# A state-space stage on Trainium2: the three-way split of the C rows done by GpSimd instead of by VectorE

## The chip, the cores and the metric

The kernel runs on one core of a Trainium2 chip. The metric is the device time of one execution in microseconds. TensorE, VectorE, ScalarE and GpSimd each work through their own list of instructions; SyncE (SP) issues the transfers between HBM and the on-chip memory SBUF. The engines meet only at semaphores.

## The reference

The program is a decoder of four layers with twelve blocks, over 128 sequences of 64 rows of 128 numbers. The change lies in one block, the attention slot of layer 2, which is a two-way state-space model ("mamba"), one pass forward and one over the reversed sequences. One pass is

```python
xz = einsum('bld,ed->ble', x, in_w); xs, z = split(xz, 2)
xs = silu(conv(xs) + conv_b)                       # 4 taps
dt, Bc, Cc = split(einsum('bld,ed->ble', xs, xproj_w), [8, 24])
dt = softplus(einsum('blr,dr->bld', dt, dt_w) + dt_b)
A = -exp(Alog)
dA  = exp(dt[..., None] * A)                       # 16 states
dBx = dt[..., None] * Bc[:, :, None, :] * xs[..., None]
h[t] = dA[t] * h[t-1] + dBx[t]
y[t] = sum over the states of h[t] * C[t]
out = ((y + Dp * xs) * silu(z)) @ out_w.T
```

## The kernel before

The stage is the function `mamba`. It treats 512 rows (eight sequences) at a time, called a group, with the 256 inner channels as two halves of 128 partitions. There are 16 groups to a pass and two passes, so 32 groups in one run of loops; `par` is the parity of a group. `group` on each engine goes over the states s = 3 to 15 of group i and then over states 0 to 2 of group i + 1; beside the states of group i, the preparation (`front`) of group i + 1 is done a piece at a time.

For each state GpSimd multiplies dt * xs (`dtx`) by the state's row of B, spread over all partitions, into `dBx` (`state`, L2602 to L2612; the multiplication is at L2600). ScalarE makes the decays exp(dt * A) (L2824), one of the two halves at a time, in three slots of PSUM. VectorE runs the recurrence over both halves (`scan`, L2957 to L2966), and multiplies the result by the row of C (`weigh`, L2976). TensorE spreads the row of C over the partitions in `ps_C` (L2700), and adds up the weighed states in `ps_y` (L2719). `dBx` has four slots: GpSimd waits before state s until state s - 4 is scanned. ScalarE may be three halves ahead of the scan.

The C rows reach TensorE as three bf16 parts whose sum is the fp32 row, so that the product with a matrix of ones and zeros is exact in bf16. The way is: ScalarE writes the low-rank products `low` (L2855, at its state 5); SP stores them in HBM (L2532) and loads the C rows as `piece`, 128 partitions of 64 (L2535); `split_rows` forms the three parts (L2947 to L2955); SP stores them (L2539) and loads them as `parts` (L2542); TensorE first needs them for state 0 of the next group, in its step of state 15. SP's order for a group is: store and load of the rows (`store_rows`), B rows of the state pairs 0 and 1, the parts (`load_parts`), B rows of the pairs 2 to 7 (`spread_B`, each of which waits for GpSimd's products).

`SPLIT` is 8. VectorE does, in its group i, scan 8, weigh 7, and then `split_rows(i + 1)`, then scan 9.

GpSimd's `front` for group i + 1 adds x and ln at s = 11 (L2620, waiting for ScalarE's ln of L2870), then v + e (L2624), v * r, dt + v (L2630) and dtx, each behind the product of a state. The sequence on ScalarE that leads to it is: relu and exp after the decays of state 8 (L2863, L2865), v and ln after the decays of state 9 (L2868, L2870). At the first state of the next group VectorE needs GpSimd's first product, which needs dtx.

Between the two passes (`turnover`) VectorE also scales the other pass's taps (L2927) after state 10 of one group, and makes two diagonal matrices (L2932) after state 10 of the next.

Of the kernel before, what the change touches and what calls it, by code (L numbers as in the profile page):

```python
# [66 lines left out]
class Scope:  # L67
# [15 lines left out]
    def sb(self, name, shape, dt=F32):  # L83
        if name in self.weights:
            return self.weights[name]
        return self.ctx.enter_context(self.nc.sbuf_tensor(f"{self.name}_{name}", shape, dt))
# [4 lines left out]
    def sem(self, name):  # L91
        self.sems.append(self.nc.alloc_semaphore(name=f"{self.name}_{name}"))
        return self.sems[-1]


def bc(ap, shape):
    return ap.to_broadcast(shape)
# [1216 lines left out]
def rows(t, i):  # L1314

    return t[:, bass.ds(i * TPG, TPG), :]
# [1147 lines left out]
def mamba(C, name, W, BC_rows, part_rows):  # L2464
# [5 lines left out]
    nc = C.nc  # L2470
# [5 lines left out]
    SKIPPED, SPLIT, PIECE = 6, 8, NS * GT // P  # L2476
    FREE_HALVES, FREE_STATES, FREE_ROWS = 3, SLOTS * CHUNK, 1
    with ExitStack() as ctx:
# [16 lines left out]
        piece, rest, split = sb("piece", [P, PIECE]), sb("rest", [P, PIECE]), sb("split", [P, 3, PIECE], BF16)  # L2495
# [12 lines left out]
        dbl_done, piece_loaded, split_ready = sem("dbl_done"), sem("piece_loaded"), sem("split_ready")  # L2508
# [80 lines left out]
        @block.gpsimd  # L2589
        def _(pool):  # L2590
            nc.gpsimd.memset(hT[:], 0.0).then_inc(prepared, 1)
            nc.gpsimd.memset(dBx[:], 0.0).then_inc(dBx_ready, FREE_STATES)
            pool.drain()

            def hold():

                pool.sem_inc(begun, 1)

            def multiply(to, one, other):
                return nc.gpsimd.tensor_tensor(to, one, other, ALU.mult)  # L2600

            def state(j, s, par, in_prologue=False):  # L2602

                slot = s // CHUNK % SLOTS
                if s % CHUNK == 0:
                    pool.wait_ge(B_loaded[slot], j * 32 + (s // FREE_STATES * 16 + 16))
                if s >= BX or not in_prologue:
                    pool.wait_ge(scanned, j * (2 * NS) + (2 * s - 2 * BX + 2 + FREE_HALVES))
                hold()
                halves = lambda t: t.rearrange("p m t -> p t m")  # L2610
                multiply(halves(dBx[:, s % BX, :, :]), halves(dtx[:]),
                         bc(Bs[:, slot, s % CHUNK, :].unsqueeze(2), [P, GT, NHF])).then_inc(dBx_ready, 1)  # L2612

            def front(j, s, par):


                if s == 11:
                    pool.wait_ge(ln_ready, j + 1)
                    hold()
                    nc.gpsimd.tensor_tensor(dt[:, par, :, :], x[:], ln[:], ALU.add)  # L2620
                elif s == 12:
                    pool.wait_ge(excess, j + 1)
                    hold()
                    nc.gpsimd.tensor_tensor(v[:], v[:], e[:], ALU.add)  # L2624
                    pool.drain()
                elif s == 13:
                    multiply(v[:], v[:], r[:])
                    pool.drain()
                elif s == 14:
                    nc.gpsimd.tensor_tensor(dt[:, par, :, :], dt[:, par, :, :], v[:], ALU.add).then_inc(dt_ready, 1)  # L2630
                    pool.drain()
                elif s == 15:
                    pool.drain()
                    multiply(dtx[:], dt[:, par, :, :], xs[:, par, :, :])
                    pool.drain()

            for s in range(11, 16):
                front(0, s, 0)
            for s in range(AHEAD):
                state(0, s, 0, True)  # L2640
            with pool.Fori(0, C.NG) as pair:
                for par in range(2):
                    i = pair * 2 + par
                    for s in range(AHEAD, NS):
                        state(i, s, par)
                        front(i + 1, s, 1 - par)
                    for s in range(AHEAD):
                        state(i + 1, s, 1 - par)
# [271 lines left out]
        def _(dve):  # L2920
# [3 lines left out]
            def scale_taps():  # L2924

                for k in range(NTAP):
                    last = nc.vector.tensor_tensor(taps[:, k, :], taps[:, k, :], in_w[:, 0:DI], ALU.mult)  # L2927
                return last

            def diagonals(second):  # L2930
                for m in range(NHF):
                    last = nc.vector.tensor_scalar(diagD[:, m, :], C.ident[:], Dp[:, second, m:m + 1], None, ALU.mult)  # L2932
                return last
# [10 lines left out]
            nc.vector.tensor_scalar(A[:], A[:], -1.0, None, ALU.mult).then_inc(prepared, 1)  # L2944
            dve.drain()

            def split_rows(j):  # L2947

                dve.wait_ge(piece_loaded, j * 16 + 16)
                nc.vector.tensor_copy(split[:, 0, :], piece[:])  # L2950
                dve.drain()
                nc.vector.tensor_tensor(split[:, 1, :], piece[:], split[:, 0, :], ALU.subtract)
                nc.vector.tensor_tensor(rest[:], piece[:], split[:, 0, :], ALU.subtract)
                dve.drain()
                nc.vector.tensor_tensor(split[:, 2, :], rest[:], split[:, 1, :], ALU.subtract).then_inc(split_ready, 1)  # L2955

            def scan(j, s, in_prologue=False):  # L2957
                if s >= HS or not in_prologue:
                    weighed = (s - HS) % NS
                    back = 1 if s < HS else 0  # L2960
                    dve.wait_ge(yc_ready, j * NDW + (weighed + 1 - back * NDW + FREE_ROWS))
                dve.wait_ge(dBx_ready, j * NS + (s + 1 + FREE_STATES))
                for m in range(NHF):
                    dve.wait_ge(decay, j * (2 * NS) + (2 * s + m + 1))
                    nc.vector.tensor_tensor_scan(hs[:, s % HS, m, :], ps_dA[:, (2 * s + m) % 3, :], dBx[:, s % BX, m, :], 0.0,  # L2965
                                                 ALU.mult, ALU.add).then_inc(scanned, 1)  # L2966

            def weigh(j, s, wait_free=True):
                if s in POOL_WEIGHS:
                    return  # L2970
                rank = DVE_WEIGHS.index(s)
                dve.wait_ge(scanned, j * (2 * NS) + (2 * s + NHF + FREE_HALVES))
                if wait_free:
                    dve.wait_ge(y_added, j * NS + (DVE_WEIGHS[rank - 2] + 1 - (NS if rank < 2 else 0)))
                dve.wait_ge(C_done, j * NDW + (rank + 1))
                nc.vector.tensor_tensor(yc[:, rank % 2, :, :], hs[:, s % HS, :, :], bc(ps_C[:].unsqueeze(1), both),  # L2976
                                        ALU.mult).then_inc(yc_ready, 1)

            split_rows(0)
            for s in range(AHEAD):  # L2980
                scan(0, s, True)
                if s:
# [2 lines left out]
            def group(i, par, second, turnover=False):  # L2985

                for s in range(AHEAD, NS):
                    scan(i, s)
                    weigh(i, s - 1)
                    if s == SPLIT:  # L2990
                        split_rows(i + 1)
                    if turnover and par == 0 and s == SPLIT + 2:
                        dve.wait_ge(taps_loaded, 32)
                        scale_taps().then_inc(taps_ready, 1)
                    if turnover and par == 1 and s == SPLIT + 2:
                        dve.wait_ge(y_added, i * NS + (SKIPPED + 1))
                        diagonals(1).then_inc(diag_ready, 1)
                scan(i + 1, 0)
                weigh(i, NS - 1)
                scan(i + 1, 1)  # L3000
                dve.wait_ge(y_added, i * NS + NS)
                nc.vector.tensor_tensor(q[:], sz[:, par, :, :], ps_y[:], ALU.mult).then_inc(y_ready, 1)
                weigh(i + 1, 0)
                scan(i + 1, 2)
                weigh(i + 1, 1)
                dve.wait_ge(out_done, i + 1)
                if not second:
                    dve.wait_ge(Y_ready, i + 1)
                at = rows(C.Y, i - SECOND if second else i)
                nc.vector.tensor_tensor(at, ps_j[:].rearrange("p (t d) -> p t d", d=D), at, ALU.add).then_inc(out_read, 1)  # L3010

            with dve.Fori(*LOOPS[0]) as pair:
                for par in range(2):
                    group(pair * 2 + par, par, False)
            for par in range(2):
                group(SECOND - 2 + par, par, False, True)
# [1277 lines left out]
```

## Time and profile before

| what | value |
|---|---|
| median of three runs | 7302.22 us (7290.1 to 7309.01) |
| span of the profiled execution | 7292.4 us |
| the stage of the change | about 2290 to 4160 us of the span, 32 groups |
| busy share of the whole span | TensorE 89%, VectorE 74%, ScalarE 56%, GpSimd 39% |

The profile is of one execution. For each instruction the trace has its start, its duration, its line and its tiles, and the idle time of its engine before it with what ended it. POOL is GpSimd, DVE is VectorE, ACT is ScalarE, PE is TensorE and SPq is the DMA queue of SP. The tiles of the stage are named with m_ in front. "issue" is a wait for nothing that the profile shows.

### The profile page before, as it was taken

Reading aid. Unit: us, or ns where it says so; the run is one execution under the profiler, and the core shown is the slowest. Engines: PE = TensorE matmul, PEld = TensorE weight load, DVE = VectorE, ACT = ScalarE, POOL = GpSimd, SP = SyncE. Lnnn points to the kernel's source line nnn. Section 1 sums busy time; section 2 is a strip of 40 time slices with the busy share of each in tenths; the row PEclk is TensorE's granted clock in tenths of the full one; section 3 lists DMA queues with packets and bytes.
Section 4 is the critical chain, followed back from the end, with each engine's and each line's share of the span. In section 5 each row is a group of like instructions: output and inputs, shape, how many; then the busy total and the mean of one; then the engine's idle time right before and its main releaser. Section 6 shows DMA issues by size and latency. Waiting matters only on the chain. (4 is left out here: it accounts for less than half of the span.)

```text
span 7292.4 us, 189527 instructions
## 1 busy us (share of the span) xinstructions
PE 6507.4 (89%) x74836; PEld 3973.7 (54%) x74836; DVE 5360.5 (74%) x8933; ACT 4055.2 (56%) x6024; POOL 2820.5 (39%) x1680
## 2 busy tenths in 40 slices
PE   7989987887697989989999779989899999989998
PEld 5767665444442333333333356666576767667676
DVE  7877576665556999999999856677577777768544
ACT  3556343665446777777777745455344444456433
POOL 3321175332214888888888601165021212211000
PEclk9999978999888999999999989999999999999999
DMA  1000000000001222222222100000000000000000
GB/s 29 0 21 13 3 11 8 3 3 2 14 2 52 76 73 75 75 80 77 76 75 76 51 12 13 9 31 3 12 2 2 2 2 2 2 15 14 2 0 23
DMA packets 115881, 190.04 MB, mean 26 GB/s; under 512 B 38661, under 2 KB 74746, under 8 KB 114970
## 3 DMA queue, kind: packets, MB, share of 16 engines
q1 hardware_dynamic: 112218, 183.47, 7.9%
q8 instruction: 337, 5.52, 0.3%
q10 hardware_dynamic: 3264, 0.54, 0.1%
q14 instruction: 62, 0.51, 0.0%
HBM read 173.87 MB, written 7.98 MB: 25 GB/s over the span
## 5 line engine op out<-in xcount | busy, mean ns | idle before, releaser
L2600 POOL TENSOR_TENSOR m_dBx<-m_dtx,m_Bs 128x1024 f32<-128x1024 f32 x515 | 1165.8, 2283 | 227.3 <-DVE m_hs L2965 185.2
L2965 DVE TENSOR_TENSOR_SCAN m_hs<-m_ps_dA,m_dBx 128x512 f32<-128x512 f32 x1030 | 1200.5, 1207 | 56.4 <-POOL m_dBx L2600 55.8
L2719 PE MATMUL m_ps_y<-m_yc,ident 128*128 128x512 f32 x2060 | 1021.6, 619 | 0.0
L2824 ACT ACTIVATE m_ps_dA<-m_dt,m_A 128x504 f32<-128x504 f32 x1030 | 682.0, 678 | 427.1 <-DVE m_hs L2965 424.4
L2096 POOL TENSOR_TENSOR a_s<-a_s,a_den 128x1024 f32<-128x1024 f32 x128 | 243.5, 1902 | 1123.9 <-DVE a_den L2142 1123.9
L2976 DVE TENSOR_TENSOR m_yc<-m_hs,m_ps_C 128x1024 f32<-128x1024 f32 x515 | 616.3, 1197 | 1.3 <-PE m_ps_C L2700 1.3
L2719 PEld LDWEIGHTS m_ps_y<-m_yc,ident 128*128 128x128 f32 x2060 | 350.5, 190 | 357.0 <-issue 357.0
L2700 PE MATMUL m_ps_C<-m_parts,m_sel 48*128 48x512 bf16 x516 | 199.8, 387 | 175.7 <-DVE m_yc L2976 175.6
L2700 PEld LDWEIGHTS m_ps_C<-m_parts,m_sel 48*128 48x128 bf16 x516 | 47.7, 92 | 566.9 <-DVE m_yc L2976 421.2
L625 POOL TENSOR_TENSOR c_kbd<-c_kf,c_hmask 128x1024 f32<-128x1024 f32 x66 | 125.0, 1893 | 515.9 <-ACT c_kf L534 492.0
L2140 DVE TENSOR_REDUCE a_den<-a_s 128x16 f32<-128x1024 f32 x128 | 156.0, 1219 | 207.0 <-ACT a_s L2047 207.0
L1930 PEld LDWEIGHTS a_ps_out<-a_wo,a_oT 128*128 128x128 f32 x2048 | 238.3, 192 | 102.9 <-ACT a_oT L2051 102.9
L1653 PEld LDWEIGHTS f_ps_o<-f_w,f_hid 128*128 128x128 f32 x2048 | 246.4, 192 | 66.0 <-issue 46.1
L1930 PE MATMUL a_ps_out<-a_wo,a_oT 128*128 128x128 f32 x2048 | 261.0, 281 | 10.8 <-ACT a_oT L2051 1.1
L1682 ACT ACTIVATE f_hid<-f_ps_h 128x1024 f32<-128x1024 f32 x128 | 129.4, 1023 | 247.7 <-PE f_ps_h L1644 247.5
L2096 POOL TENSOR_TENSOR c_s<-c_s,c_den 128x1024 f32<-128x1024 f32 x32 | 60.9, 1902 | 514.3 <-DVE c_den L2142 514.3
L1730 DVE SCALAR_TENSOR_TENSOR f_acc<-f_ps_o,f_cw,f_acc 128x128 f32<-128x128 f32 x384 | 108.1, 344 | 203.7 <-PE f_ps_o L1653 203.7
L1653 PE MATMUL f_ps_o<-f_w,f_hid 128*128 128x128 f32 x2048 | 250.9, 276 | 7.2 <-ACT f_hid L1682 7.2
L1644 PE MATMUL f_ps_h<-f_xnT,f_w 128*128 128x512 f32 x512 | 241.6, 600 | 0.0
L2043 ACT ACTIVATE a_pT<-a_ps_t 128x1024 f32<-128x1024 f32 x128 | 130.7, 1021 | 141.4 <-PE a_ps_t L1905 141.4
L3732 POOL TENSOR_TENSOR x_qk<-x_qk,x_spread 128x1024 f32<-128x1024 f32 x36 | 85.2, 2367 | 307.7 <-ACT x_spread L3607 307.7
L2027 ACT ACTIVATE a_qT<-a_ps_j 128x512 f32<-128x512 f32 x129 | 77.0, 597 | 219.6 <-PE a_ps_j L1860 219.5
(748 smaller groups left out, 16025.2 us busy)
## 6 DMA issues: line engine op xcount, KB each, us to landing
m_Bs<-BC_rows SPq DMA_DIRECT2D x258, 512.0 KB, 3.5
c_kvb<-in_ctxT SPq DMA_DIRECT2D x68, 128.0 KB, 2.1
c_kvb<-in_ctxT SPq DMA_DIRECT2D x17, 256.0 KB, 2.7
out_dram<-X SPq DMA_DIRECT2D x1, 4096.0 KB
BC_rows<-m_low SPq DMA_DIRECT2D x33, 64.0 KB, 2.7
part_rows<-m_split SPq DMA_DIRECT2D x33, 48.0 KB, 1.7
m_parts<-part_rows SPq DMA_DIRECT2D x33, 48.0 KB, 1.7
m_piece<-BC_rows SPq DMA_DIRECT2D x33, 32.0 KB, 1.7
```

Of the source, the lines that this page charges most:

```text
L1644: last = nc.tensor.matmul(ps_h[:, e % 2, c, :], w1[:, e, c * P:(c + 1) * P], fr.xnT[:], start=True, stop=True)
L1653: last = nc.tensor.matmul(ps_o[:, e % 2, p * D:(p + 1) * D], hid[:, e % 2, c, p * P:(p + 1) * P], w2[:, e, c, :], start=(c == 0), stop=(c ...
L1930: last = nc.tensor.matmul(ps_out[:, UT * u + t, :], oT[:, t, j, :], wo[:, t, hg * NJ + j, :], start=hg == 0 and u == 0 and t == 0 and j == ...
L2043: nc.scalar.activation(pT[:].rearrange("p t j q -> p t (j q)"), ps_t[:], ACT.Copy).then_inc(pT_ready, 1)
L2096: nc.gpsimd.tensor_tensor(s1[:, par, :, :, :], s1[:, par, :, :, :], bc(den[:, par, :, :].unsqueeze(3), [P, UT, UH, S]), ALU.mult).then_inc ...
L2140: nc.vector.tensor_reduce(den[:, par, :, :], s1[:, par, :, :, :], AX, ALU.add)
L2600: return nc.gpsimd.tensor_tensor(to, one, other, ALU.mult)
L2700: nc.tensor.matmul(ps_C[:], sel[0:3 * NS, s, :], parts[0:3 * NS, par, :], start=True, stop=True).then_inc(C_done, 1)
L2719: last = nc.tensor.matmul(ps_y[:, m, :], C.ident[:], of[:, m, :], start=s == 0, stop=s == NS - 1)
L2824: nc.scalar.activation(seqs(ps_dA[:, h % 3, :]), seqs(dt[:, par, m, :]), ACT.Exp, scale=A[:, second, m, s:s + 1]).then_inc(decay, 1)
L2965: nc.vector.tensor_tensor_scan(hs[:, s % HS, m, :], ps_dA[:, (2 * s + m) % 3, :], dBx[:, s % BX, m, :], 0.0, ALU.mult, ALU.add).then_inc(s ...
L2976: nc.vector.tensor_tensor(yc[:, rank % 2, :, :], hs[:, s % HS, :, :], bc(ps_C[:].unsqueeze(1), both), ALU.mult).then_inc(yc_ready, 1)
```

## The change

The function `split_rows` goes from VectorE's block to GpSimd's, with the same four operations, now with `hold()` (an increment of a semaphore that nobody waits for) behind its wait. VectorE's calls, one before the loops and one after weigh 7 of each group, are removed. GpSimd calls it before its first work and, in each group, in `front` at s = 8, that is behind its product of state 8 and ahead of that of state 9. `SPLIT` stays 8; as GpSimd is ahead of VectorE by up to four states, the place is another moment in time.

```diff
+            def split_rows(j):
+
+                pool.wait_ge(piece_loaded, j * 16 + 16)
+                hold()
+                nc.gpsimd.tensor_copy(split[:, 0, :], piece[:])
+                pool.drain()
+                nc.gpsimd.tensor_tensor(split[:, 1, :], piece[:], split[:, 0, :], ALU.subtract)
+                nc.gpsimd.tensor_tensor(rest[:], piece[:], split[:, 0, :], ALU.subtract)
+                pool.drain()
+                nc.gpsimd.tensor_tensor(split[:, 2, :], rest[:], split[:, 1, :], ALU.subtract).then_inc(split_ready, 1)
+
             def front(j, s, par):
 
-
+                if s == SPLIT:
+                    split_rows(j)
                 if s == 11:
...
+            split_rows(0)
             for s in range(11, 16):
                 front(0, s, 0)
...
-            def split_rows(j):
-
-                dve.wait_ge(piece_loaded, j * 16 + 16)
-                nc.vector.tensor_copy(split[:, 0, :], piece[:])
-                dve.drain()
-                nc.vector.tensor_tensor(split[:, 1, :], piece[:], split[:, 0, :], ALU.subtract)
-                nc.vector.tensor_tensor(rest[:], piece[:], split[:, 0, :], ALU.subtract)
-                dve.drain()
-                nc.vector.tensor_tensor(split[:, 2, :], rest[:], split[:, 1, :], ALU.subtract).then_inc(split_ready, 1)
-
...
-            split_rows(0)
             for s in range(AHEAD):
                 scan(0, s, True)
...
                     weigh(i, s - 1)
-                    if s == SPLIT:
-                        split_rows(i + 1)
```

## Rows read from the trace of the kernel before

**Rows 1.** The page's costliest groups: line, engine, operation, tiles, count, busy, mean, idle before.

```profile
L2600 POOL TENSOR_TENSOR m_dBx<-m_dtx,m_Bs 128x1024 f32<-128x1024 f32 x515 | 1165.8, 2283 | 227.3 <-DVE m_hs L2965 185.2
L2965 DVE TENSOR_TENSOR_SCAN m_hs<-m_ps_dA,m_dBx 128x512 f32<-128x512 f32 x1030 | 1200.5, 1207 | 56.4 <-POOL m_dBx L2600 55.8
```

**Rows 2.** Busy time by engine in ten stretches of the stage, their sum.

```profile
sum 1860.00, PE 1687.38 PEld 656.88 DVE 1809.77 ACT 1420.13 POOL 1530.40; mean PE 168.74 PEld 65.69 DVE 180.98 ACT 142.01 POOL 153.04
```

**Rows 3.** Waits of VectorE, 2290 to 4150: total us, times, longest.

```profile
DVE m_hs L2965 <- POOL m_dBx L2600: 37.1, 30, 1.3
```

**Rows 4.** Timeline, VectorE, one group: start, duration, instruction, count, idle before.

```profile
3009.70 2.33 DVE L2965 TENSOR_TENSOR_SCAN m_hs<-m_ps_dA,m_dBx 128x512 f32<-128x512 f32 x2
...
3013.06 0.19 DVE L2950 CAST m_split<-m_piece 128x64 bf16<-128x64 f32 x1
...
3013.95 2.34 DVE L2965 TENSOR_TENSOR_SCAN m_hs<-m_ps_dA,m_dBx 128x512 f32<-128x512 f32 x2
...
3034.12 2.33 DVE L2965 TENSOR_TENSOR_SCAN m_hs<-m_ps_dA,m_dBx 128x512 f32<-128x512 f32 x2
...
3038.78 2.34 DVE L2965 TENSOR_TENSOR_SCAN m_hs<-m_ps_dA,m_dBx 128x512 f32<-128x512 f32 x2 [1.22 <-POOL m_dBx L2600]
```

**Rows 5.** Timeline, GpSimd, the same group; the first row is state 8.

```profile
2998.85 2.29 POOL L2600 TENSOR_TENSOR m_dBx<-m_dtx,m_Bs 128x1024 f32<-128x1024 f32 x1 [1.15 <-DVE m_hs L2965]
...
3014.19 2.36 POOL L2620 TENSOR_TENSOR m_dt<-m_x,m_ln 128x1024 f32<-128x1024 f32 x1 [3.05 <-ACT m_ln L2870]
...
3036.37 15.68 POOL L2600 TENSOR_TENSOR m_dBx<-m_dtx,m_Bs 128x1024 f32<-128x1024 f32 x7 [0.39 <-issue]
```

**Rows 6.** Timeline, ScalarE, the same group: the decay of state 8 and ln.

```profile
3007.59 0.69 ACT L2824 ACTIVATE m_ps_dA<-m_dt,m_A 128x504 f32<-128x504 f32 x1 [0.92 <-DVE m_hs L2965]
...
3012.95 1.06 ACT L2870 ACTIVATE m_ln<-m_v 128x1024 f32<-128x1024 f32 x1
```

**Rows 7.** Tile m_split, 2290 to 4150: count, duration min/median/max in ns, first and last start.

```profile
L2950 DVE CAST m_split<-m_piece x32: 184/186/191, 2316.5 to 4121.5; 128x64 bf16<-128x64 f32 x32
```

**Rows 8.** Between the passes: all of L2927, then timelines of GpSimd and VectorE.

```profile
L2927 DVE TENSOR_TENSOR m_taps<-m_taps,m_in_w x8: 412/423/2554, 2241.9 to 3140.1; 128x256 f32<-128x256 f32 x8
...
3136.69 5.97 DVE L2927 TENSOR_TENSOR m_taps<-m_taps,m_in_w 128x256 f32<-128x256 f32 x4
...
3139.87 2.51 POOL L2600 TENSOR_TENSOR m_v<-m_v,m_r 128x1024 f32<-128x1024 f32 x1
...
3166.55 1.22 DVE L3002 TENSOR_TENSOR m_e<-m_sz,m_ps_y 128x1024 f32<-128x1024 f32 x1 [0.58 <-PE m_ps_y L2719]
...
3218.62 2.34 DVE L2965 TENSOR_TENSOR_SCAN m_hs<-m_ps_dA,m_dBx 128x512 f32<-128x512 f32 x2 [0.58 <-DVE m_yc L2976]
```

**Rows 9.** Narrow GpSimd instructions of other stages: timeline, and groups of instructions.

```profile
4761.92 0.30 POOL L652 TENSOR_SCALAR f_hidden<-f_seen 128x128 bf16<-128x128 f32 x1 [0.16 <-issue]
...
L1128 POOL TENSOR_TENSOR a_feat<-a_expo,a_above 128x512 f32<-128x512 f32 x34 | 43.2, 1272 | 5.2 <-issue 4.6
...
L647 POOL TENSOR_TENSOR f_seen<-f_seen,f_tril 128x128 f32<-128x128 f32 x34 | 15.6, 457 | 5.2 <-issue 4.4
```

**Rows 10.** The piece: its transfer in two groups, landing times, and the tightest dt addition.

```profile
3001.55 0.33 SPq L2535 DMA_DIRECT2D m_piece<-BC_rows  x1
...
3014.01 0.37 SPq L2539 DMA_DIRECT2D part_rows<-m_split  x1
...
DMA to landing us min/median/max: 1.6/1.7/1.9
...
3587.98 0.32 SPq L2535 DMA_DIRECT2D m_piece<-BC_rows  x1
...
3600.26 2.35 POOL L2620 TENSOR_TENSOR m_dt<-m_x,m_ln 128x1024 f32<-128x1024 f32 x1 [3.03 <-ACT m_ln L2870]
```

**Rows 11.** Timeline ahead of the loops, VectorE's first split and GpSimd's first addition.

```profile
2267.70 0.20 DVE L2950 CAST m_split<-m_piece 128x64 bf16<-128x64 f32 x1 [21.03 <-DMA m_piece<-BC_rows]
...
2272.60 2.35 POOL L2620 TENSOR_TENSOR m_dt<-m_x,m_ln 128x1024 f32<-128x1024 f32 x1 [32.38 <-ACT m_ln L2870]
```

## Prediction

> **What bounds the kernel now.** I read the page first, then the waits of the stage, then one group of the stage instruction by instruction on each engine, and last the few rows that price small GpSimd instructions. The page puts the two costliest GpSimd and VectorE loops of the whole program into this stage [rows 1]. Here VectorE works 1809.8 of 1860 us and GpSimd 1530.4 [rows 2], so VectorE looks like the bound and taking work from it looks like a gain. The waits say something finer: VectorE stands still 37.1 us in 30 places, each time for a dBx that GpSimd has not finished, at most 1.3 us [rows 3]. There are 32 groups; 30 of them hold one such wait.
>
> One group shows where. VectorE runs scan, weigh, scan, weigh without a gap to state 15 (3034.12), and then the next group's state 0 starts at 3038.78 after 1.22 us of waiting for GpSimd [rows 4]. GpSimd's own line shows the opposite pattern [rows 5]: through state 11 it waits about 1.1 us before every product because it may be only four states ahead of the scans; then it waits 3.05 us for ScalarE's ln; and from 3014.19, where ln releases it, it runs dt, v, dtx and the products of states 12 to 15 nearly back to back until dBx of the next group's state 0 is there at 3036.37 + 2.28 = 3038.65. VectorE starts 0.13 us later. So each group has two parts. From the first scan to the first half of state 7's scan VectorE sets the pace. That half releases ScalarE at 3007.59 [rows 6]; two relu, two exp of states, v and ln follow on ScalarE, ln ends at 3014.01, and from there GpSimd's chain of 3038.65 - 3014.19 = 24.5 us sets the pace. VectorE only accompanies that second part and arrives 1.22 us early.
>
> **Where the split stands in this.** On VectorE it begins at 3013.06, after weigh 7, and ends where scan 9 starts at 3013.95 [rows 4]: 0.89 us, four instructions and two drains. That is in the second part, behind scan 7, which releases the path, and beside the path. All 32 groups have it, on average 58.2 us apart ((4121.5 - 2316.5) / 31 [rows 7]).
>
> **Removed.** 32 x 0.89 = 28.5 us of VectorE time in the loop, and 0.9 us ahead of it, in a stretch where VectorE otherwise waits for GpSimd's first products. In an ordinary group scans 9 to 15 come 0.89 us earlier. The latest of the products is dBx 15: counted back from 3036.37 over the gap of 0.39, dtx (2.36 like the addition of 3014.19) and a gap of 0.16 behind a drain, it ends at about 3033.5, and scan 15 would come at 3034.12 - 0.89 = 3033.23, so some 0.3 us of waiting appears there; the earlier products have more room. The next scan cannot start before 3038.65 + 0.13 whatever VectorE does. What is late next is the same GpSimd product as now, only the wait grows from 1.22 to about 2.1 us (shared between scan 15 and the next scan 0). Gain of an ordinary group: 0. The later work of the group (out, Y, weigh 15) comes after that scan on VectorE, so it does not move either.
>
> Two groups are unlike the others, those between the two passes. In one, 5.97 us of tap scaling lengthen VectorE's line and no wait for GpSimd is left; the waits there are short ones for TensorE (0.58 us at 3166.55 [rows 8]), whose convolution waits for these very taps. There the 0.89 us come off the path. The other is about even: the next scan 0, at 3218.62, comes after an idle 0.58 us already, so it has arrived early too. I count 0.9 us in all.
>
> **Added, on GpSimd.** After dBx 8: a wait for the DMA of the piece, one cast, three subtractions of 128x64, two drains. None of these is in the trace on this engine. The nearest rows [rows 9]: a tensor_tensor of 128x128 took 0.457 us and one of 128x512 1.272 us, so 2.12 ns a column and, extrapolated, an estimated 0.32 us at 64 columns; a write of 128x128 into bf16 took 0.298 us, and an instruction behind a drain started 0.16 us late. Hence 3 x 0.32 + 0.30 + 2 x 0.16 = 1.58 us, and 0.39 us for taking up the products again (the largest such gap, [rows 5]): 1.97 us, the value I take. Lower bound: the 0.89 us of VectorE; nothing excludes a drain at no cost but nothing makes four instructions a gain. Upper bound, all four at the 128-column price and three gaps: 4 x 0.457 + 3 x 0.16 + 0.39 = 2.7 us.
>
> **What hides it.** The piece is issued at 3001.55 and lands 1.7 us later (1.9 at most) [rows 10], so at 3003.25; GpSimd is done with dBx 8 at 3001.14 and waits 2.1 us for it. Queued behind this wait are dBx 9, 10 and 11, 3 x 2.28 = 6.85 us, and then the dt addition, due at 3014.19. The split must be over by 3007.35: 4.1 us are free, 2 are wanted. In the tightest groups the piece comes 12.28 us ahead of the dt addition (3600.26 - 3587.98 [rows 10]), and 12.28 - 1.9 - 6.85 = 3.5 us are free. So dBx 9 ends near 3007.5 instead of 3004.4; its reader, scan 9, comes at 3013.06. dBx 11 ends near 3012.1, two microseconds before ln. The cost is hidden by GpSimd's waiting for scans and for ln; if that cover went, each microsecond would cost 32 us. On SP's queue the same transfers go in the same order: B rows of state pair 0 wait for dBx 9 and go 3 us later, those of pair 1 1 us later; the stores and loads of the parts, which waited for VectorE until 3014.01, follow at once and go some 1.5 us earlier. All are wanted only about 3036 or later. ScalarE never waits for dBx. Ahead of the loops the piece is there at 2267.7 and GpSimd's first addition starts at 2272.60 [rows 11]: 2267.7 + 1.97 = 2269.7, 2.9 us to spare.
>
> **VectorE and GpSimd at once.** The split now runs beside scan 6 and weigh 6, in the part that VectorE paces, so a slowdown of the scans would cost there. Rows show that two engines can block each other: the tap scaling, whose two operands both lie in SBUF, takes 0.41 to 0.42 us alone and up to 2.55 us beside GpSimd's products, which themselves go from 2.36 to 2.51 us [rows 8]. But the scan (one operand in PSUM) takes 2.33 to 2.34 us a pair both at 3009.70, half of it beside an idle GpSimd, and at 3034.12, wholly beside a busy one [rows 4]. After the change no VectorE instruction of an ordinary group has two SBUF operands. The Trainium skill says the same (SBUF — State Buffer, section Who interferes with whom): an instruction of VectorE with two SBUF inputs contends with GpSimd's reads, one with at most one does not. The skill also warns (Perfetto Trace Analysis, Optimizing Scalar/DVE Operations) that moving work between these two might not help, as they share a port. Taken at its worst it is the third rival below.
>
> **Sum.** 7292.4 - 0.9 = 7291.5 us in the profiled execution. Its span lies between the lowest (7290.1) and the middle (7302.22) of the three timed runs, so what lies around the span is smaller than their spread and I carry the difference over: 7302.2 - 0.9 = 7301.3 us.
>
> **Rivals.** (1) VectorE is the bound after all, and GpSimd's late product moves up with it. Then 32 x 0.89 = 28.5 us are won: 7273.7. For it: VectorE's 97% in the stage. Against it: the 30 waits for GpSimd, and that GpSimd's chain starts at ln, fixed before the split. Chance 0.08. (2) Slower: the split on GpSimd outlasts the free time, the dt addition comes late, and everything up to the next group's first scan with it. It decides from 3.5 to 4.1 us a group. At 1 us an instruction and 0.16 a drain with 0.39 behind, it is 4.7 to 4.9 us; 0.8 us over, 32 times, gives +26 us: 7328. Against it: instructions of twice the columns take 0.30 and 0.46 us [rows 9]. Chance 0.06. (3) The engines block each other: each of the four instructions holds a scan or weigh up for its 0.32 us, before scan 7: 32 x 1.28 = 41 us: 7343. Against it: the constant scans. Chance 0.06. (4) Forecast, chance 0.80. That the split would not move is no case: the code has it only on GpSimd, and whether it costs GpSimd one microsecond or three, the forecast is the same.
>
> **How the numbers follow.** A measurement of this kernel can tell about 0.3%, 22 us, from no change. Rival 1 passes that on the one side, rivals 2 and 3 mostly on the other; a partial form of each end is left a little: faster 0.09, same 0.79, slower 0.12. The forecast's own range is the spread of the runs, about -11 to +8 us; I widen it toward partial forms of the rivals, 7282 to 7318, leaving out the full rivals.
>
> **What would show it.** The four instructions in GpSimd's line at about 3003 to 3005, 0.3 us each. GpSimd's idle time before the dt addition falls from 3.05 to about 2.1 us; its waits before dBx 9 to 11 vanish. VectorE busy falls by about 27 us while its wait for dBx grows from 37 to some 65 us. The groups stay 58.2 us apart on average. If they are 57.3 apart, rival 1 holds; if the dt addition shows no wait for ln, rival 2; if a scan pair is above 2.33 us near the split, rival 3.

## The result and the profile after

The changed kernel takes 7333.09 us (five runs, 7324.99 to 7339.58) against 7297.25 us (five runs, 7290.1 to 7309.01) for the kernel before on the same chip: ratio 1.0046 [1.0035, 1.0057], some 34 us slower by the ratio and 36 between the medians. The brackets hold the 95% interval; every ratio below is to the kernel before, timed along with that run. The forecast was 7301.3 us, at most 7318. It was wrong: the change costs time where it was expected to cost none.

The changed kernel's page (scan at L2968 now, decays at L2837) shows the instruction queue q14 grown from 62 packets and 0.51 MB in the kernel before (first line here), and the idle time ahead of the scan at 125.5 us where it was 56.4 [rows 1]:

```profile
q14 instruction: 62, 0.51, 0.0%
...
q14 instruction: 96, 0.79, 0.0%
...
L2968 DVE TENSOR_TENSOR_SCAN m_hs<-m_ps_dA,m_dBx 128x512 f32<-128x512 f32 x1030 | 1199.0, 1204 | 125.5 <-POOL m_dBx L2600 95.9
L2600 POOL TENSOR_TENSOR m_dBx<-m_dtx,m_Bs 128x1024 f32<-128x1024 f32 x515 | 1162.6, 2283 | 153.8 <-DVE m_hs L2968 120.6
```

An ordinary group, GpSimd's timeline, answers to [rows 5]:

```profile
3054.78 0.24 POOL L2618 CAST m_split<-m_piece 128x64 bf16<-128x64 f32 x1 [2.44 <-DMA m_piece<-BC_rows]
3055.16 0.30 POOL L2620 TENSOR_TENSOR m_split<-m_piece,m_split 128x64 bf16<-128x64 f32 x1
3055.42 0.30 POOL L2621 TENSOR_TENSOR m_rest<-m_piece,m_split 128x64 f32<-128x64 f32 x1
3055.87 0.30 POOL L2623 TENSOR_TENSOR m_split<-m_rest,m_split 128x64 bf16<-128x64 f32 x1
3056.13 6.76 POOL L2600 TENSOR_TENSOR m_dBx<-m_dtx,m_Bs 128x1024 f32<-128x1024 f32 x3
3065.49 2.36 POOL L2632 TENSOR_TENSOR m_dt<-m_x,m_ln 128x1024 f32<-128x1024 f32 x1 [2.60 <-ACT m_ln L2883]
...
3087.67 13.43 POOL L2600 TENSOR_TENSOR m_dBx<-m_dtx,m_Bs 128x1024 f32<-128x1024 f32 x6 [0.38 <-issue]
```

The split takes 1.35 us with its gaps (3054.78 to 3056.13), the three products behind it are done long before ln, and the dt addition still waits 2.60 us for it. VectorE in the same group, answering to [rows 4]:

```profile
3084.81 2.34 DVE L2968 TENSOR_TENSOR_SCAN m_hs<-m_ps_dA,m_dBx 128x512 f32<-128x512 f32 x2 [0.20 <-POOL m_dBx L2600]
...
3090.08 2.34 DVE L2968 TENSOR_TENSOR_SCAN m_hs<-m_ps_dA,m_dBx 128x512 f32<-128x512 f32 x2 [1.82 <-POOL m_dBx L2600]
```

That is the forecast's picture almost to the tenth. From one dt addition to the next I read 58.0 us in this group, as before. The loss is elsewhere. VectorE's waits from 2290 to 4150 us, answering to [rows 3] (total us, times, longest):

```profile
DVE m_hs L2968 <- POOL m_dBx L2600: 53.7, 52, 1.8
DVE m_hs L2968 <- issue: 29.0, 7, 4.3
```

The second line has no counterpart in the kernel before: seven waits of a scan for nothing that the profile shows. The first of them on VectorE's timeline:

```profile
3339.64 0.68 DVE L3010 TENSOR_TENSOR Y<-m_ps_j,Y 128x512 f32 x1
3344.61 2.34 DVE L2968 TENSOR_TENSOR_SCAN m_hs<-m_ps_dA,m_dBx 128x512 f32<-128x512 f32 x2 [4.28 <-issue]
```

The others start 120 us apart, at 3465, 3586, 3706, 3827, 3948 and 4069, each 4.0 to 4.3 us long and always ahead of the same scan, that of state 3. VectorE runs the groups in two loops with two groups a round: seven rounds for the first pass, then the two groups between the passes written out, then eight rounds for the second pass. The scan of state 3 is the first instruction with work in a round. Seven stalls are the seven re-entries of the second loop; the six of the first loop have none. They come while VectorE sets the pace, so all of their length is lost: the distances between dt additions in the second pass alternate between 58.0 and 62.1 to 63.7 us, and the seven long ones hold 32.0 us more than seven of 58.03. That is the measured loss, but for the 2 to 4 us that medians of five runs leave open. In the same stretch (3230 to 4170) q14 moved 5 packets in the kernel before and 39 here:

```profile
q14 instruction: 5, 0.04, 0.0%
...
q14 instruction: 39, 0.32, 0.1%
```

### The profile page after: what moved, and what is told of

Its sections match the earlier page's. It is cut to its first block and busy times, and to the rows that moved or that the text cites. A ratio compares the mean times of both kernels' runs of the same rounds, so it can differ in the third digit from the quotient of the medians.

```text
span 7322.9 us, 189577 instructions
## 1 busy us (share of the span) xinstructions
PE 6525.4 (89%) x74836; PEld 3976.4 (54%) x74836; DVE 5340.8 (73%) x8801; ACT 4054.1 (55%) x6024; POOL 2852.9 (39%) x1812
## 5 line engine op out<-in xcount | busy, mean ns | idle before, releaser
L2968 DVE TENSOR_TENSOR_SCAN m_hs<-m_ps_dA,m_dBx 128x512 f32<-128x512 f32 x1030 | 1199.0, 1204 | 125.5 <-POOL m_dBx L2600 95.9
L2732 PE MATMUL m_ps_y<-m_yc,ident 128*128 128x512 f32 x2060 | 1045.4, 631 | 0.0
L2837 ACT ACTIVATE m_ps_dA<-m_dt,m_A 128x504 f32<-128x504 f32 x1030 | 680.6, 678 | 457.4 <-DVE m_hs L2968 455.2
```

The source lines that it names most:

```text
L2732: last = nc.tensor.matmul(ps_y[:, m, :], C.ident[:], of[:, m, :], start=s == 0, stop=s == NS - 1)
L2837: nc.scalar.activation(seqs(ps_dA[:, h % 3, :]), seqs(dt[:, par, m, :]), ACT.Exp, scale=A[:, second, m, s:s + 1]).then_inc(decay, 1)
```

## The experiments

**The theories.** *Fetch*: VectorE's instructions come from memory through q14, in packets of 8192 bytes, which are 128 instructions if one is 64 bytes long. A loop that touches at most three such blocks stays on the chip, one that touches four is fetched again each round. I counted VectorE's instructions in the trace: a round of the second loop has 302 before and 289 after. Neither fits in two blocks (256) and both can fit in three (384), so where the loop begins within a block decides. *Rivals*: the split on GpSimd disturbs VectorE (contention, order), so that the move itself costs the 34 us; or a microsecond of either engine's time counts in full wherever it stands.

**Same work, other positions.** To the changed kernel 44 empty instructions are added, once, ahead of VectorE's first loop, where VectorE waits for GpSimd's first products in any case. The label says how many.

```diff
+            for _ in range(44):
+                dve.drain()
             for s in range(AHEAD):
                 scan(0, s, True)
```

> The changed kernel with 44 drains added on VectorE ahead of its loops, in a stretch where it waits for GpSimd's first product anyway. They put VectorE's two loops, which the change moved by 6 and 31 instructions, elsewhere in its program, and everything behind the stage where it was before the change. Theory A (code placement: the 4.0 to 4.3 us that VectorE stands still at the head of each round of its second loop, seven times, 29 us in all, is the fetching of instructions, and hangs on where the loop lies): no such wait is left and the time is that of the kernel before, less the 0.9 us once: ratio 0.999 to 1.001, some 36 us below the changed kernel. Theory B (the split on GpSimd costs the time, directly or by holding up VectorE): it stays at 7333 us, ratio 1.0046.

Measured: 7302.37 us, ratio 0.9997 [0.9988, 1.0006]. The stalls are gone and q14 is back at 62 packets. The head of the second loop, as above:

```profile
3351.03 0.68 DVE L3012 TENSOR_TENSOR Y<-m_ps_j,Y 128x512 f32 x1
3351.63 2.33 DVE L2968 TENSOR_TENSOR_SCAN m_hs<-m_ps_dA,m_dBx 128x512 f32<-128x512 f32 x2
```

The split is on GpSimd as before this edit, so the move itself costs and gains nothing that the measurement can tell (the interval is -9 to +4 us). All 32 distances between dt additions together are 1849.7 us, against 1850.1 in the kernel before.

**The border, to one instruction.** With block borders where the fetches of the changed kernel put them, 31 instructions behind the head of its second loop, 31 empty instructions make the loop start exactly on a border (128 + 128 + 33, three blocks), 30 make it start one ahead (1 + 128 + 128 + 32, four).

> The changed kernel with 31 drains ahead of VectorE's loops. Theory A, with blocks of 128 instructions: the second loop's first instruction comes to lie on the first place of a block, it spans three blocks, and the seven waits at its head are gone; stage shorter by 29 us, a span of about 7294 us. If the waits are still there, the border is not where the fetches seem to put it.

> The changed kernel with 30 drains ahead of VectorE's loops, one less than in the run beside it. Theory A, with blocks of 128 instructions: the second loop's first instruction is the last place of a block, it spans four blocks, and all seven waits of 4.0 to 4.3 us are there; a span of about 7323 us. The two runs differ in one instruction. If this one has no waits either, the count that decides is not the blocks that the loop touches.

Measured, one run each: 7299.6 us with 31, 7329.77 us with 30. Of the two pages the q14 lines, and of the second VectorE's wait, first with 31:

```profile
q14 instruction: 62, 0.51, 0.0%
```

and with 30:

```profile
q14 instruction: 97, 0.79, 0.0%
...
DVE m_hs L2968 <- issue: 29.7, 7, 4.6
```

One empty instruction, executed once, is worth 30 us, and 29.7 us of it stand in the seven waits. Contention, or the order of work on the engines, would be the same in both kernels.

**The kernel before, made slow.** The split stays on VectorE, and only positions move.

```diff
+            for _ in range(110):
+                dve.drain()
             for s in range(AHEAD):
                 scan(0, s, True)
```

> The kernel before, the split on VectorE, with 110 drains added on VectorE ahead of its loops. Theory A, with instruction blocks of 128 (8192 bytes, the size of the transfers on the instruction queue) and the block border where the changed kernel's fetches put it: the first loop (304 instructions) then lies on three blocks and the second (302) on four, so the second one waits 4.0 to 4.3 us at the head of seven rounds, 28 to 30 us in all, and the first does not: 7325 us, ratio 1.0035 to 1.0045. Theory B: the time of the kernel before, ratio 1.000.

Measured: 7316.92 us, ratio 1.0019 [1.001, 1.0028], q14 98 packets. The seven stalls are where they were expected, but 1.8 to 2.1 us long and not 4; the long groups are 2.0 us longer each, 14 us in all. That the stalls come was right and their size was wrong by half. A theory in which blocks are 256 instructions and two are held would have had no stall here: with a border where pad31 and pad30 found it, the loop starts at place 110 of a block and lies inside two of them (110 + 302 = 412, below 512). What could make the size: in this kernel 18 instructions are left in the block in which the loop starts, enough to begin work as soon as that one block is there. In pad30 one is left, so two blocks have to come, one after the other. In the changed kernel 31 are left, but its last block holds 2 instructions, so its fetch may still be on the way at the jump back. That was a guess made from three runs, and the next run was to test it, on both loops at once.

How many packets come in a stall can be read from the queue. A packet starts about 0.3 us before the last instruction of a round ends; then, in the changed kernel, a second one starts within the 4.28 us of the wait (3340.0 to 3344.6), and in before_pad110 none does until the scan has begun (3347.7 to 3349.9):

```profile
q14 instruction: 2, 0.02, 1.8%
...
q14 instruction: 1, 0.01, 1.3%
```

> The kernel before with 84 further empty instructions (drains) ahead of VectorE's first loop; no work of the stage is changed. Theory A (code of VectorE is fetched in blocks of 128 instructions, a border at loop position 45 before its first loop; a loop that touches four blocks is fetched anew each round; the length of a stall is the number of blocks that have to come before the first scan, one of them if the loop starts well inside its block, two if only few instructions of the first block are left or the border fetch is still under way): the second loop (302 instructions) starts at place 84 and ends at 386, beyond 384, so seven stalls; the first (304) starts at place 106 and ends at 410, so seven stalls too, now in the first pass as well. Both start within 44 instructions of their block's end: 1.9 us a stall if that is enough for the next block to come in time, 4.2 if not: 14 x 1.9 = 27 us (ratio 1.004) to 14 x 4.2 = 59 us (1.008); my guess 7 x 4.2 + 6 x 1.9 = 41 us (1.0055). Packets of the instruction queue go from 62 to some 128. Theory B (the stalls hang on the second loop alone, whatever the position of the first): seven stalls in the second pass, none in the first, at most 29 us (1.004), packets 97.

Measured: 7351.86 us, ratio 1.0064 [1.0047, 1.008], q14 127 packets. VectorE's timeline, one head of the first loop and one of the second, and its waits for nothing shown:

```profile
2662.10 2.34 DVE L2965 TENSOR_TENSOR_SCAN m_hs<-m_ps_dA,m_dBx 128x512 f32<-128x512 f32 x2 [1.80 <-POOL m_dBx L2600]
...
3495.31 2.34 DVE L2965 TENSOR_TENSOR_SCAN m_hs<-m_ps_dA,m_dBx 128x512 f32<-128x512 f32 x2 [4.06 <-issue]
...
DVE m_hs L2965 <- issue: 28.9, 7, 4.3
```

The second loop (44 + 128 + 128 + 2) stalls 4.0 to 4.3 us at its seven re-entries, the first (22 + 128 + 128 + 26) 1.8 to 2.7 us at its six. 28.9 us and six groups that are 1.9 to 2.8 us longer, 13 us together, make 42 where 41 were guessed. Over all 32 distances between dt additions the kernel is 44 us longer, inside the 34 to 58 us of the interval. The rival, that only the second loop can stall, falls. The thirteen stalls have the packets of the two before: one before the scan in each of the six short ones, two in each of the seven long ones. The stalls of the first loop carry labels of other releasers (here GpSimd's dBx): the profile's "issue" finds only the longer ones.

The loops that tell most, with the number of instructions that fall in each block (the other loops of these kernels lie on three blocks and have no stall):

| kernel, loop | instructions by block | stall at each re-entry |
|---|---|---|
| before, 1 and 2 | 106+128+70; 128+128+46 | none |
| after, 1 | 112+128+51 | none |
| after, 2 | 31+128+128+2 | 4.0 to 4.3 us |
| pad44, 2 | 115+128+46 | none |
| pad31, 2 | 128+128+33 | none |
| pad30, 2 | 1+128+128+32 | 4.1 to 4.6 us |
| before_pad110, 2 | 18+128+128+28 | 1.8 to 2.1 us |
| before_pad84, 1 | 22+128+128+26 | 1.8 to 2.7 us |
| before_pad84, 2 | 44+128+128+2 | 4.0 to 4.3 us |

The Trainium skill (Runtime: NRT & Kernel Launch, section Instruction fetch mechanics) says that an engine's instructions are held in two blocks of 16 KiB, 256 instructions each, and that a taken branch to a block not held waits for its fetch. The second half is what the runs show. The first is not, for VectorE: its packets are half that size, and loops over three of them ran without a fetch.

**Is the split free on either engine?** With positions repaired, the split is done twice and four times on GpSimd (`for n in range(2)` or `range(4)` around the four operations).

> The changed kernel with the 44 drains, and the split done twice on GpSimd in each group. One split with its gaps takes 1.35 us here; the dt addition still waits 2.4 to 2.9 us for ln. Theory (GpSimd's chain begins at ln, and all that fits ahead of it is free): the second split fits, wait for ln falls to about 1.1 to 1.5 us, ratio 1.000, groups 58.0 us apart. Rival (a microsecond of GpSimd's time costs a microsecond wherever it stands, or disturbs VectorE's scans beside it): 32 x 1.35 = 43 us, ratio 1.006.

> The changed kernel with 44 drains ahead of VectorE's loops, and with the split's four operations done four times in a row on GpSimd. One split took 1.35 us there (3054.78 to 3056.13 in the changed kernel), and with it 2.4 to 2.8 us were left before the dt addition. Theory A (a split costs nothing while it fits in GpSimd's waiting, and everything beyond): three more are 3 x 1.35 = 4.0 us, 1.2 to 1.6 us beyond the room, in some 31 groups 37 to 50 us: ratio 1.005 to 1.007. Theory B (a split on GpSimd always costs what it takes): 3 x 1.35 x 32 = 130 us, ratio 1.018. Theory D (GpSimd has room for it all): ratio 1.000.

Twice: 7308.02 us, ratio 1.0007 [0.9997, 1.0016], nothing within the measurement. Four times: 7373.21 us, ratio 1.0097 [1.0082, 1.0113]. GpSimd's timeline, first twice and then four times:

```profile
3014.84 2.37 POOL L2634 TENSOR_TENSOR m_dt<-m_x,m_ln 128x1024 f32<-128x1024 f32 x1 [1.33 <-ACT m_ln L2885]
```

```profile
3043.64 6.77 POOL L2600 TENSOR_TENSOR m_dBx<-m_dtx,m_Bs 128x1024 f32<-128x1024 f32 x3
3050.34 2.39 POOL L2634 TENSOR_TENSOR m_dt<-m_x,m_ln 128x1024 f32<-128x1024 f32 x1
```

The second split comes out of the wait for ln, which falls by its length from 2.6 to 1.3 us. It is free but for a small rest: the 32 distances are 4.1 us longer together than in pad44, 2.2 of them in the first three, where a full price would be 43. With four the wait is gone: that is the second rival of the prediction, here brought about. Three further splits are 4.0 us, 1.4 more than the wait that covers them, so 32 x 1.4 = 45 us. The run lost 71. VectorE's wait for the output sum grew as well, here 2.23 us long where it is 0.6 at most in pad44:

```profile
3082.86 1.22 DVE L3006 TENSOR_TENSOR m_e<-m_sz,m_ps_y 128x1024 f32<-128x1024 f32 x1 [2.23 <-PE m_ps_y L2734]
```

Its total is 36.3 us against 7.2 in pad44, and 45 and 29 are 74. The two hold group by group as well: in the 29 ordinary groups the distance beyond 58.03 us is the growth of this wait plus 1.1 to 1.8 us. TensorE comes late because it is slow there. Its timeline ahead of that wait, and the same four products of pad44 at 3105.45:

```profile
3078.52 0.60 PE L2715 MATMUL m_ps_C<-m_parts,m_sel 48*128 48x512 bf16 x1 [2.85 <-DVE m_yc L2981]
3079.05 3.78 PE L2734 MATMUL m_ps_y<-m_yc,ident 128*128 128x512 f32 x4
...
3105.45 1.98 PE L2732 MATMUL m_ps_y<-m_yc,ident 128*128 128x512 f32 x4
```

From 3078.4 to 3082.8 the granted clock of TensorE is 0.50, its lower level of 1.2 GHz, after it stood idle for 2.85 us; from 3069 to 3076 it was 1.00, and in pad44 it is 1.00 at these products in every group, after an idle time of 1.6 us at most. Seven of the 29 groups of pad44_four kept 1.00 there, and in them VectorE waited 0.22 us as in pad44. So what outlasts the cover on GpSimd costs more than its own length here.

**The split twice on VectorE**, in the kernel before, was to double the removed term.

```diff
-                nc.vector.tensor_copy(split[:, 0, :], piece[:])
+                for n in range(2):
+                    nc.vector.tensor_copy(split[:, 0, :], piece[:])
                     ...
```

> The kernel before with the four operations of the split done twice in a row on VectorE, so 0.89 us more in each of 32 groups. By the count of instructions its two loops (316 and 314 long) lie on three blocks each, so no wait at their heads. Theory A, with the reading that from ln on GpSimd's chain sets the pace: VectorE's wait of 1.22 us for the next group's first dBx shrinks to some 0.3 us and the time moves by nothing but 0.9 us between the passes: ratio 1.000. Theory C (VectorE sets the pace everywhere): 28 us slower, ratio 1.0038.

Measured: 7443.22 us, ratio 1.0197 [1.0181, 1.0213], with no stall of fetch (q14 62). Both theories had said 28 us or less, and it was 141. VectorE's timeline (the first split is over at 3003.06) and GpSimd's first addition:

```profile
3003.06 0.19 DVE L2951 CAST m_split<-m_piece 128x64 bf16<-128x64 f32 x1
3003.32 0.23 DVE L2953 TENSOR_TENSOR m_split<-m_piece,m_split 128x64 bf16<-128x64 f32 x1
3003.47 2.37 DVE L2954 TENSOR_TENSOR m_rest<-m_piece,m_split 128x64 f32<-128x64 f32 x1
3005.91 2.15 DVE L2956 TENSOR_TENSOR m_split<-m_rest,m_split 128x64 bf16<-128x64 f32 x1
...
3003.35 2.41 POOL L2620 TENSOR_TENSOR m_dt<-m_x,m_ln 128x1024 f32<-128x1024 f32 x1 [3.06 <-ACT m_ln L2870]
```

As soon as GpSimd begins its chain, a subtraction of VectorE lasts until GpSimd's instruction ends: 2.37 us for one that takes 0.22 alone. The groups are 62.3 us apart or somewhat more where they were 58.05, and 32 x 4.3 = 137 us. In the kernel before the split ends at 3013.95 and ln releases GpSimd at 3014.19 [rows 4, 5]. It is cheap there because it is over 0.24 us before GpSimd's work begins.

**ln one state earlier.** In an ordinary group of the changed kernel VectorE waits 0.2 + 1.8 us for GpSimd's chain, which hangs on ln. ScalarE's relu and exp move to its state 7, v and ln to state 8, v and r to state 9, in the kernel before and in pad44.

```diff
-                elif s == 8:
                     act.drain()
                     for m in range(NHF):
...
-                elif s == 9:
+                elif s == 8:
...
-                elif s == 10:
+                elif s == 9:
```

> The kernel before with ScalarE's preparation steps one state earlier: relu and exp right behind the two abs of state 7 (instead of behind state 8), v and ln at state 8, v and r at state 9. ln then ends some 2.2 us earlier, just when GpSimd is done with dBx 11. Theory A (ln and GpSimd's chain behind it set the pace of the group's second part): the chain starts about 2.1 us earlier, VectorE waits for no dBx any more and sets the pace; won are its waits, 1.22 us in 30 groups, 37 us: ratio 0.995. Theory C (VectorE paces already): no gain, ratio 1.000.

> The changed kernel (split on GpSimd) with 44 drains ahead of VectorE's loops, and with ScalarE's preparation steps one state earlier as in the run beside it. Theory A: GpSimd, with the split ahead of dBx 9, is done with dBx 11 about when ln is there; the chain starts some 2.0 us earlier, and VectorE, 0.89 us a group shorter, has waited 2.04 us: won are about 2.0 us in 30 groups, 58 to 62 us, ratio 0.9915 to 0.992. The difference to the run beside it, about 25 us, is then what moving the split is worth where VectorE sets the pace. If the two come out alike, GpSimd or TensorE has become the limit at once.

Measured: with the split on VectorE 7453.6 us, ratio 1.0205 [1.0191, 1.0219], where 0.995 was expected; with the split on GpSimd 7267.21 us, ratio 0.995 [0.9936, 0.9963], the fastest of all and below both kernels of the case. Theory A of the first run failed for the reason seen in before_twice: all but the last of the split's instructions now lie beside GpSimd's chain and last until GpSimd's instruction ends. Tile m_split in before_early (min/median/max ns):

```profile
L2949 DVE CAST m_split<-m_piece x33: 195/1356/1371, 2275.3 to 4273.1; 128x64 bf16<-128x64 f32 x33
L2951 DVE TENSOR_TENSOR m_split<-m_piece,m_split x33: 225/2183/2192, 2275.6 to 4274.3; 128x64 bf16<-128x64 f32 x33
L2952 DVE TENSOR_TENSOR m_rest<-m_piece,m_split x33: 219/2375/2378, 2275.7 to 4276.4; 128x64 f32<-128x64 f32 x33
```

and in pad44_early GpSimd's dt addition and VectorE's waits in the stage:

```profile
3005.71 2.37 POOL L2632 TENSOR_TENSOR m_dt<-m_x,m_ln 128x1024 f32<-128x1024 f32 x1 [0.43 <-ACT m_ln L2882]
...
DVE m_hs L2967 <- POOL m_dBx L2600: 42.1, 2, 40.7
DVE m_e L3003 <- PE m_ps_y L2732: 13.0, 31, 0.6
DVE m_yc L2978 <- PE m_ps_C L2713: 7.2, 16, 0.6
```

The waits for dBx are gone from the loop (40.7 of the 42.1 us are the one before it) and VectorE is the bound: 56.4 us from one dt addition to the next instead of 58.03. More was expected, 58 to 62 us, and 35 came. Most groups win 1.6 us, as the 2.0 us of waits give way to some 0.4 for TensorE. Nine win 0.7 to 0.9 only, with a wait of 0.5 to 0.6 us for the spread C row in each of them, and the two groups between the passes are 3.4 us longer together, their tap scaling lasting 7.21 us and the diagonals 3.12, now on the path. So what the move buys is room: with the early ln it is the difference between 7453.6 and 7267.2 us.

The Trainium skill (SBUF — State Buffer, section Who interferes with whom) says that a VectorE instruction with two SBUF inputs contends with a GpSimd instruction that reads SBUF, and that of two contenders the later one waits for the whole of the other. The subtractions of before_twice and before_early do just that. The cast, with one input, lasts 1356 ns instead of 195, which fits what the section says of casts in a two-port mode.

## Why the prediction was wrong, point by point

- **What bounds an ordinary group**: right. Groups stay 58.0 us apart, and VectorE's waits for dBx are the 0.3 us ahead of scan 15 (measured 0.20) and, ahead of the next scan 0, 2.1 less 0.3 (measured 1.82). Their total grew from 37.1 us to 53.7 only (48.4 in pad44, from 2300 us on), not to 65: in about half of the groups a part of the freed time goes into waits for the spread C row (ps_C) instead, 0.7 us in all before and 9.9 in pad44. That was not forecast, and it costs nothing as long as GpSimd is the later one.
- **Removed, 0.89 us a group beside the path**: right as engine time, gain 0. pad44 has it alone, at ratio 0.9997.
- **Added, 1.97 us on GpSimd**: mis-sized, 1.35 measured. The subtractions took 0.30 us each and the cast 0.24, close to the 0.32 and 0.30 of the extrapolation; 0.39 us for taking up the products again was too much, as the next product starts with no gap.
- **What hides it**: right. The free time of 3.5 to 4.1 us holds two splits (pad44_two) and not four (pad44_four), so the point from which the second rival decides was sound. The wait for the piece was 2.44 us (2.1 forecast), the one ahead of the dt addition 2.60 (2.1).
- **VectorE and GpSimd at once**: right for the scans, 2.33 us a pair beside the split. But the paragraph looked only at what the moved split would meet on GpSimd and not at what it met on VectorE.
- **0.9 us won between the passes**: wrong, if small. The tap scaling comes earlier and lies more fully beside GpSimd's products: 6.82 us in pad44 where [rows 8] have 5.97. The two distances there sum to 121.85 us in pad44 and 121.74 before.
- **The sum**: here is the step that failed. It took the instructions taken off VectorE as time and nothing else. They are also places in VectorE's list: its rounds shrank from 304 and 302 instructions to 291 and 289, and the second loop's head moved from a block's border to 31 instructions ahead of one. 29.0 us of stalls, 32.0 with what follows them in the groups, are the excess, up to the 2 to 4 us that medians of five runs leave open. No rival held this mechanism, and the three that there were, at 7273.7, 7328 and 7343, all fell. That rival 2's time is near the measured one is chance: it rests on a wrong reason, since the dt addition still waits 2.60 us for ln.

The page of the kernel before could have warned: q14 is on it with 62 packets, VectorE's loops can be counted in the trace, and at 302 instructions a loop that fits three blocks from one start and needs four from most others was there to be seen. Which of the two the change would bring could not be read from it without the size and the borders of the blocks.

## What to carry to other kernels

Count the instructions of an engine's loop before and after a change, not only their time: on VectorE the loops measured here, of 289 to 304 instructions, were safe or not depending on where they start, and the sign is a rise of the instruction queue's packets together with waits for nothing shown at the head of each round. When a change that should be neutral costs a few tenths of a per cent, shift the code with a few empty instructions before any other explanation is believed. A small two-input instruction of VectorE that sits just ahead of GpSimd's next work is a trap for whatever would make that work start earlier, and here moving it to GpSimd paid only with that second step. And work hidden in an engine's waiting is free up to the length of that wait; beyond it, the delay can slow another engine too.

## What the runs showed of the hardware

- VectorE's instructions come in packets of 8192 bytes. Loops that touch three blocks ran without any fetch, loops that touch four were fetched again every round, about five packets each time (34 to 36 more for seven re-entries, 65 more for thirteen). A stall is 1.8 to 2.7 us where one packet starts before the first scan and 4.0 to 4.6 us where two do, the second 1.8 to 2.6 us after the round's end. Why one loop needs a second packet (few instructions left in its first block, or a fetch at its end still on the way) is a model that forecast before_pad84, and no row shows it.
- A stall of fetch can carry the label of another releaser: the thirteen of 1.8 to 2.7 us are all put down to GpSimd or ScalarE, the 4 us ones to "issue".
- On GpSimd a subtraction of 128x64 took 304 ns and a cast into bf16 236 ns, against 218 to 226 and 186 on VectorE.
- VectorE's subtraction of 64 columns beside GpSimd's work lasted 2.15 to 2.38 us, and a cast 1.36 us: each until the GpSimd instruction beside it ended.
- TensorE's granted clock fell from 1.00 to 0.50 after it had stood idle for 2.85 us (pad44_four), and four products took 3.78 us instead of 1.98.
